# Softmax times V in column groups of 32 instead of 64, with the softmax sums formed apart from it

## The reference, cut to what matters

```python
x = _layernorm(x + _L0_attn_ref(x, W_qkv, b_qkv))          # rotary self-attention, 16 heads of 32, full softmax
x = _layernorm(x + _L0_xattn_ref(x, ctx, ctx, ...))        # 12 gathered nodes of a tree over the context
x = _layernorm(x + _L0_ffn_ref(x, w1, b1, w2, b2))         # 512 -> 2048 -> 512, ReLU
```

```python
scores = jnp.einsum('bhqd,bhkd->bhqk', q, k) / math.sqrt(D)
w = jax.nn.softmax(scores, axis=-1)
out = jnp.einsum('bhqk,bhkd->bhqd', w, v)
```

## Time and profile before

| | us |
|---|---|
| median of 3 runs (2359.38 to 2368.48) | 2360.6 |
| the profiled execution | 2362.72 |
| its span, first to last instruction | 2360.7 |
| TensorE busy | 2049.5 (87%) |
| VectorE busy | 1616.1 (68%) |
| ScalarE busy | 1072.2 (45%) |
| GpSimd busy | 1036.9 (44%) |

### The profile page before, as it was taken

One profiled execution on the slowest core, in us unless ns is written; L12 is line 12 of the kernel. 1 busy time (PEld: TensorE's weight loads), 2 busy tenths in 40 slices (PEclk: granted clock), 3 DMA queues, 4 the chain that ended last, 5 costly groups with the idle time before them and its releaser, 6 DMA issues.

```text
span 2360.7 us, 33037 instructions
## 1 busy us (share of the span) xinstructions
PE 2049.5 (87%) x11360; PEld 1023.6 (43%) x11360; DVE 1616.1 (68%) x2129; ACT 1072.2 (45%) x1854; POOL 1036.9 (44%) x1084
## 2 busy tenths in 40 slices
PE   4899999999999999996147888998989999988997
PEld 2333333333333333331014555555555555555555
DVE  8564647566564647552568888888888888888850
ACT  3354545455555545464013444444444444444444
POOL 3232534244352535233444464465555555455420
PEclk9999999999999999998568999999999999999999
DMA  5442434434342434331875675665665675675520
GB/s 193 146 126 73 144 97 131 145 108 152 121 149 79 142 96 130 117 108 63 311 268 186 220 235 188 220 231 199 221 236 195 215 255 195 206 249 195 199 85 18
DMA packets 188800, 392.40 MB, mean 166 GB/s; under 512 B 20692, under 2 KB 82260, under 8 KB 188632
## 3 DMA queue, kind: packets, MB, share of 16 engines
q1 hardware_dynamic: 133336, 188.91, 25.1%
q0 software_dynamic: 55296, 201.35, 24.6%
HBM read 312.33 MB, written 77.59 MB: 165 GB/s over the span
## 4 chain that ended last, share of the span: by engine, by line
DVE 28%; DMA 11%; POOL 5%; issue 4%; PE 3%; ACT 0%; DVEq 0%; SPq 0%; ACTq 0%; POOLq 0%
DMA nb<-kv_flat,idx_rows 10%; DVE bank L1497 10%; DVE logits L1444 5%; POOL nb L1568 5%; DVE nb L1493 5%; DVE nb L1435 4%; PE bank L1172 1%; PE bank L1148 1%; DMA own<-kv_flat 1%; DVE bank L1503 1%; DVE logits L1448 1%; DVE own L1439 1%; DVE total L1474 1%; DVE top L1466 1%; DVE weights L1481 0%
## 5 line engine op out<-in xcount | busy, mean ns | idle before, releaser
L712 DVE TENSOR_REDUCE neg_max<-rows_ps 128x2 f32<-128x1024 f32 x256 | 312.4, 1220 | 298.3 <-PE rows_ps L499 298.2
L1568 POOL DMA_INDIRECT nb<-kv_flat,idx_rows x384 | 366.6, 955 | 138.0 <-issue 86.2
L1435 DVE TENSOR_TENSOR nb<-nb,bank 128x1024 f32<-128x1024 f32 x192 | 231.7, 1218 | 142.5 <-DMA nb<-kv_flat,idx_rows 137.7
L627 ACT ACTIVATE probsT<-e_ps 128x1024 f32<-128x1024 f32 x256 | 262.0, 1023 | 145.1 <-PE e_ps L527 144.8
L1596 POOL TENSOR_TENSOR nb<-nb,weights 128x1024 f32<-128x1024 f32 x96 | 182.5, 1914 | 281.8 <-DVE weights L1481 281.1
L1497 DVE TENSOR_TENSOR bank<-bank,nb 128x512 f32<-128x512 f32 x384 | 268.2, 698 | 24.7 <-DVE bank L1497 0.5
L1148 PE MATMUL bank<-x2T_hi,w_hi_sb 128*128 128x256 f16 x1024 | 282.4, 276 | 0.7 <-issue 0.7
L1148 PE MATMUL bank<-x2T_lo,w_hi_sb 128*128 128x256 f16 x1024 | 281.9, 275 | 0.0
L1148 PE MATMUL bank<-x2T_hi,w_lo_sb 128*128 128x256 f16 x1024 | 281.4, 275 | 0.0
L517 PE MATMUL o_ps<-probsT,v_sb 128*33 128x512 f32 x1024 | 269.6, 605 | 6.3 <-ACT oT L624 6.1
L1444 DVE TENSOR_REDUCE logits<-nb 128x32 f32<-128x1024 f32 x192 | 230.0, 1211 | 0.0
(11 more groups left out here) (158 smaller groups left out, 3611.8 us busy)
## 6 DMA issues: line engine op xcount, KB each, us to landing
kv_flat<-kv_nat SPq DMA_DIRECT2D x128, 256.0 KB, 3.3
own<-kv_flat SPq DMA_DIRECT2D x32, 512.0 KB, 3.8
q_stack<-qk_dram SPq DMA_DIRECT2D x96, 128.0 KB, 3.0
k_stack<-qk_dram SPq DMA_DIRECT2D x96, 128.0 KB, 3.3
piece<-in_pieces SPq DMA_DIRECT2D x40, 256.0 KB, 3.5
in_sb<-in_xT SPq DMA_DIRECT2D x8, 1024.0 KB, 6.6
in_sb<-in_ctxT SPq DMA_DIRECT2D x8, 1024.0 KB, 5.6
qk_dram<-hi SPq DMA_DIRECT2D x32, 256.0 KB, 2.2
```

Source lines behind the costliest of these rows:

```text
L627: act.activation(probsT[:, (d - E_LAG) % TT, :, :], e_ps[:], ACT.Exp, scale=1.0 / (Q_UP * K_UP))\
L712: dve.tensor_reduce(neg_max[:, g % 2, at:at + 2], rows_ps[:], AX.X, ALU.max, negate=True).then_inc(max_done, 1)
L1435: dve.tensor_tensor(kk, kk, q.unsqueeze(1).to_broadcast([P, GN, D]), ALU.mult)\
L1568: pool.indirect_dma_start(nb[:, slot(lt, g), k, :], None, kv_flat, bass.IndirectOffsetOnAxis(idx_rows[:, lt, at:at + 1], 0))\
```

## The change

The product with V takes four heads (a "quad") side by side, each with weights of 32 columns at partitions 0, 32, 64 and 96 of `o_ps`, in every second step. The exponentials of a quad's four key blocks come in the order block by block, two steps each. The column of ones is gone. The softmax sums are formed apart: the exponentials of the four key blocks are added up, in place in the buffer of one block, GpSimd adding the second block (128x2048, in steps 0, 8, 16 and 24) and VectorE the third and fourth (steps 2, 4, 10, 12, 18, 20, 26, 28). A new aux item "sum" (steps 5, 13, 21, 29) multiplies the result with 32 columns of ones, four heads side by side; ScalarE copies it (`sumT`), and one step later ("share") four fp32 matmuls with four columns of the identity turn it into the layout of the queries, of which VectorE takes the reciprocal. The step after that is the output turn, now once per quad, four per sequence. `probsT` holds three buffers of one block of four heads.

To make room in memory the rotation is done in place (`rot` is gone), so its first product waits for the shuffle and ScalarE's `raw` waits for GpSimd's low part; the tree's output has two buffers (`NAT`) instead of four. The tables of steps are rewritten: aux items, bounces, splits, normalisation, residual. The tail has 27 steps.

```diff
-TAIL = 25
+ADD_LAG = E_LAG + 4
+SUM_LAG = V_LAG + 7
+SHARE_LAG = SUM_LAG + 1
+OUT_LAG = SHARE_LAG + 1
+PROBS_PLACE = ((0, 1, 2, 1), (2, 1, 0, 1))
+TAIL = 27
-NAT = 4
+NAT = 2
-BOUNCE_NEXT = {12: 0, 16: 1, 25: 2, 31: 3}
+BOUNCE_NEXT = {11: 0, 15: 1, 29: 2, 31: 3}
-STACK_NEXT = {21: 0, 29: 1}
-X_SPLIT, CTX_LOAD, CTX_SPLIT, X_LOAD = 4, 12, 20, 25
-X1_SPLIT = {18: (0,), 19: (1,), 22: (2, 3)}
-X1_STORE, X_ROWS_LOAD, X_ROWS_BIAS = (20, 24), 24, 27
-RESIDUAL = 15
-LN_STEPS = {16: (("stats", 0), ("stats", 1)), 17: (("apply", 0), ("stats", 2)),
-            18: (("apply", 1), ("stats", 3)), 19: (("apply", 2), ("apply", 3))}
+STACK_NEXT = {21: 0, 30: 1}
+X_SPLIT, CTX_LOAD, CTX_SPLIT, X_LOAD = 2, 10, 22, 27
+X1_SPLIT = {20: (0,), 22: (1,), 24: (2, 3)}
+X1_STORE, X_ROWS_LOAD, X_ROWS_BIAS = (23, 26), 26, 30
+RESIDUAL = 16
+LN_STEPS = {17: (("stats", 0), ("stats", 1)), 19: (("apply", 0), ("stats", 2)),
+            21: (("apply", 1), ("stats", 3)), 23: (("apply", 2), ("apply", 3))}
+AUX_AT = {0: (("kv", 0),), 2: (("kv", 1),), 3: (("kv", 2),), 4: (("kv", 3),), 5: (("sum", 2),), 6: (("qk", 0),),
+          8: (("qk", 1),), 9: (("tree", 0), ("tree", 1)), 10: (("qk", 2),), 11: (("tree", 2), ("tree", 3)),
+          12: (("qk", 3),), 13: (("tree", 4), ("tree", 5), ("sum", 3)), 14: (("v", 0),),
+          15: (("tree", 6), ("tree", 7)), 16: (("kv", 4),), 17: (("kv", 5),), 18: (("kv", 6),), 19: (("v", 1),),
+          20: (("kv", 7),), 21: (("sum", 0),), 22: (("v", 2),), 23: (("v", 3),), 24: (("qk", 4),),
+          25: (("tree", 8), ("tree", 9)), 26: (("qk", 5),), 27: (("tree", 10), ("tree", 11)), 28: (("qk", 6),),
+          29: (("tree", 12), ("tree", 13), ("sum", 1)), 30: (("qk", 7),), 31: (("tree", 14), ("tree", 15))}
...
+                    elif kind == "sum":
+                        pe.wait_ge(probs_added, START + 2 * (b * QUADS + (i if i < 2 else i - QUADS) + 1))
+                        for side in range(QUAD):
+                            mm = pe.matmul(o[side * DH:(side + 1) * DH, :], ones[:],
+                                           probsT[:, PROBS_PLACE[i % 2][0], side, :], start=True, stop=True)
...
-                            for side in range(2):
-                                mm = pe.matmul(O[side * SIDE:side * SIDE + VW, :],
-                                               v_sb[:, slot, kt, 2 * pair + side, :],
-                                               probsT[:, (d - V_LAG) % TT, side, :], start=kt == 0, stop=kt == TT - 1)
+                            for side in range(QUAD):
+                                mm = pe.matmul(O[side * DH:(side + 1) * DH, :],
+                                               v_sb[:, slot, kt, quad % QUADS * QUAD + side, :],
+                                               probsT[:, PROBS_PLACE[quad % 2][kt], side, :],
+                                               start=kt == 0, stop=kt == TT - 1)
...
+                            for t in range(TT):
+                                mm = pe.matmul(MB[:, t * QUAD:(t + 1) * QUAD], sumT[:, t * P:(t + 1) * P], heads,
+                                               start=True, stop=True)
...
+                            if kt < 2 and side == 0 and not (first and quad == 0):
+                                act.wait_ge(probs_added, START + 2 * n - 1 + kt)
+                            if kt == 3 and side == 0:
+                                act.wait_ge(first_added, START + n + 1)
...
+                            dve.wait_ge(e_done, START + n * PER_CHUNK + 2 * kt + 2)
+                            if kt == 2:
+                                dve.wait_ge(first_added, START + n + 1)
+                            else:
+                                dve.wait_ge(probs_added, START + 2 * n + 1)
+                            summed = probsT[:, place[0]].rearrange("p h t -> p (h t)")
+                            dve.tensor_tensor(summed, summed, probsT[:, place[kt]].rearrange("p h t -> p (h t)"),
+                                              ALU.add).then_inc(probs_added, 1)
...
+                            pool.wait_ge(e_done, START + n * PER_CHUNK + 4)
+                            pool.wait_ge(probs_used, START + 3 * n + 1)
+                            summed = probsT[:, place[0]].rearrange("p h t -> p (h t)")
+                            pool.tensor_tensor(summed, summed, probsT[:, place[1]].rearrange("p h t -> p (h t)"),
+                                               ALU.add).then_inc(first_added, 1)
```

More of the change, by code:

```diff
@@ L60 @@
 ROW_SCALE = 4096.0
-ONES = DH
-VW = DH + 1
-SIDE = 64
 M_ROW = 3 * DH
@@ L68 @@
 GROUP = 16
-PAIRS = H // 2
+QUADS = H // 4
+QUAD = 4
 STEPS = TT * H // 2
@@ L97 @@
[L97 to L121, removed]
-    before = 2 * KC if first else len(aux_order(True, False)) + 2 * KC - len(aux_order(False, False))
-    return before + (0 if first else b * len(aux_order(False, False))) + aux_place(kind, i, first, last)
+STACK_NEXT = {21: 0, 30: 1}
@@ new lines, with aux_items, aux_order @@
+V_FIRST = {0: (0, 1), 1: (2,), 2: (3,)}
+def aux_items(d, first, last, tail=False):
+    own = tuple(("v0", i) for i in V_FIRST.get(d, ())) if first else ()
+    late = d < SUM_LAG
+    return own + tuple(item for item in AUX_AT.get(d, ())
+                       if not (last and item[0] in ("qk", "v")) and not (first and item[0] == "sum" and late)
+                       and not (tail and (item[0] != "sum" or not late)))
+def aux_order(first, last, tail=False):
+    return [item for d in range(STEPS) for item in aux_items(d, first, last, tail)]
@@ new lines, in aux_place, with aux_number @@
+def aux_place(kind, i, first, last, tail=False):
+    return aux_order(first, last, tail).index((kind, i))
+def aux_number(b, kind, i, first, last, tail=False):
+    whole = len(aux_order(False, False))
+    if first:
+        behind = 2 * KC
+    elif tail:
+        behind = 2 * KC + len(aux_order(True, False)) + (b - 2) * whole + len(aux_order(False, True))
+    else:
+        behind = 2 * KC + len(aux_order(True, False)) - whole + b * whole
+    return behind + aux_place(kind, i, first, last, tail)
@@ L140, in max_group, with share_turn @@
     return (d // PER_CHUNK - 1) % KC
+def share_turn(d, first, tail):
+    return quad_step(d, SHARE_LAG, first, tail)
 def out_turn(d, first, tail):
-    return d % TT == V_LAG % TT and not (first and d < V_LAG + TT) and not (tail and d > V_LAG)
+    return quad_step(d, OUT_LAG, first, tail)
 def misc_order(first, tail):
-    return [(kind, d) for d in range(TAIL if tail else STEPS) for kind, turn in (("max", max_turn), ("out", out_turn))
+    return [(kind, d) for d in range(TAIL if tail else STEPS) for kind, turn in (("max", max_turn), ("share", share_turn), ("out", out_turn))
             if turn(d, first, tail)]
@@ L521, in iteration @@
+                        for kind, i in aux_items(d, first, last, tail):
+                            if kind == "sum":
+                                aux(b, kind, i, first, last, tail)
                         if e_step(d, first, tail):
-                            pair, kt = divmod((d - E_LAG) % STEPS, TT)
+                            quad, at = divmod((d - E_LAG) % STEPS, PER_CHUNK)
+                            kt, pair = at // 2, 2 * quad + at % 2
                             if (d - E_LAG) % PER_CHUNK == 0:
```

134 lines of the change are left out of this document (76 added, 58 removed).

## The result

The changed kernel took 2349.6 us (median of six runs, 2333.5 to 2354.4), the kernel before beside it 2363.3: ratio 0.9922, 95% interval 0.9899 to 0.9945. The same file in a second job gave 2343.5 against 2357.7: 0.9936 (0.9911 to 0.996). So it is faster, by about 14 us; the forecast was 36.

What follows compares the result with a forecast made beforehand. TensorE's own instructions were taken to set the pace. Six steady periods -31 us, iteration 0 -4, last iteration -6, tail +5: total -36, from a median of 2360.6 to 2325 us, range 2275 to 2382.

Steps and rivals of the forecast that it cites:

- The product's pitch: TensorE's product with V: four heads side by side at a pitch of 1.05 us, against 0.98 for two.
- rival 4: TensorE's column groups run two and two, product 1.96 us, period 141, total 2428 us; chance 0.07.
- the period: One steady batch: 116.0 us of TensorE work plus 11 of stalls, 127.0 against 132.1.
- the walk of steps 9 to 13: Stalls of 1.1 us before step 9, 0.6 before 11, 0.5 before 12, 1.0 before 13, together 3.2.
- the three meetings with GpSimd in steps 23, 25 and 31: GpSimd delays VectorE: 1.5 us for normalisations of 23, 1.2 for the rotation of 25, 1.1 for that of 31.
- Rival 3: GpSimd's additions hold VectorE's two-input operations: 143 us a batch, +63 in all, half of it 2375; chance 0.12.
- rival 1: VectorE's slack takes in rotations and additions, stalls stay at 6 us: period 122, total 2290; chance 0.12.
- Rival 2: Gain just eaten: stalls of 15 to 19 us a batch, total within 12 us of the median; chance 0.09.
- The walk: Step by step through a batch: rotations and additions in neighbouring steps stall TensorE by 3.2, 3.6 and 1.0 us.
- Last iteration, -6 forecast: Last iteration: steps without a projection held at 1.96 us by the maximum's loop, so not -10 but -6 us.
- None comes near: SP queue moves, including stores with two buffers for four: nothing charged; stores land after 3.3 us, tree-turn pairs 6 apart.
- Tail, +5 forecast: Tail: addition, sum, its copy and share behind the last exponential, 2.2 + 1.1 + 0.6 + 0.9, about +5 us.

Runs made afterwards that it cites:

- run 4: Changed kernel with all twelve additions of exponentials per sequence cut to 16 of 2048 columns, waits kept: 2308.1 us, 0.9784.
- run 3: Changed kernel with the last sequence's load of x's rows behind the last tree stores and its bias in step 1 of the tail: 2337.1 us, 0.9909.
- run 8: Changed kernel with mended ends: loads as in run 3, VectorE making all three tail additions, GpSimd's bias waiting for the first quad's: 2330.8 us, 0.9857.
- run 12: Mended ends of run 8 plus unread row scores in the tail, behind the scores of steps with a product: 2328.4 us, 0.9881.
- Run 2: Kernel before the change with two buffers for the tree's output instead of four, nothing else: 2388.4 us, 1.0132.
- the first kind of fill: Unread row scores in the tail, placed ahead of the products: 2326.8 us, 0.9882 with mended ends; 2336.4 us, 0.9923 with the change's own ends.
- run 7: Changed kernel with only GpSimd's additions cut to 16 columns: 2315.4 us, 0.9835; with only VectorE's cut: 2311.0 us, 0.9809.

## Why the prediction was wrong in size

**Right.** The product's pitch (1.00 for 1.05, rival 4 is out), the sums and shares, VectorE's addition (2.3 where nothing holds it), the period (126.2 and 127.1 for 127.0), iteration 0, the walk of steps 9 to 13, and the three meetings with GpSimd in steps 23, 25 and 31. Rival 3 is out, as no period came near 133; rival 1 too, since VectorE's slack didn't swallow anything. Rival 2 came near in the total, but not by its cause: stalls were 11.6 us a batch, not 15 to 19. GpSimd's addition took 4.56 for 4.1. In rival 4 the terms as written add up to 2433, not 2428.

**Right, but not additive.** The walk charged 7.8 us of stalls to rotations and additions side by side, and run 4 finds 8.1 at the steps of the additions. Yet without them the period is only 3.5 us shorter: behind these stalls stand others, above all the tree's two buffers, which they cover. The normalisations of step 23 were taken at 1.5 and cost 2.3.

**Last iteration, -6 forecast, +7 measured.** Two steps failed. "None comes near", said of the SP queue, took a store's landing to be 3.3 us, the median. A store behind a load of 1 MB frees its buffer later: in the last iteration the load of x stands ahead of four stores, TensorE waits 5.5 us for the sum's buffer (which the prediction named as a sign of being wrong), and the loss is 6 to 7.5 us (runs 3 and 8), less where TensorE comes later (run 12). Run 2 shows that the term deserved a price anywhere. The other 5.5 us: even mended it gains nothing (95.9 for 96.2). The -6 counted no hold by GpSimd there, but step 23 with its normalisations takes 5.2 us where the kernel before has 2.7, and step 25 is 1.6 longer. It also took the clock to stay at 1.00, and the mended last iteration has 0.95. How the 5.5 us divide among these isn't shown.

**Tail, +5 forecast, +10.5 measured.** The forecast put its +5 behind the last exponential and nothing ahead of it. Us from the last maximum to the last exponential, and from there to the first gather:

| | to the last exponential | behind it | clock up to it |
|---|---|---|---|
| before | 22.8 | 33.8 | 1.00 |
| forecast | 22.8 | 38.8 | 1.00 |
| after | 30.3 | 36.9 | 0.82 |
| mended ends (8) | 28.7 | 39.1 | 0.82 |
| mended ends, tail filled (12) | 25.6 | 37.2 | 1.00 |

Behind the last exponential the chain came to +3.1, less than forecast. The step that failed is one that was never written down: that the exponentials of the tail keep their old pace, and TensorE its clock of 1.00. They came 7.5 us later. Part of it is there at clock 1.00 too (2.8 us in the filled tail). Part is half clock: scores, products, sum and turns on the chain take about double, 5 us in the mended tail (run 12). Part is GpSimd's additions, for which two exponentials of after wait, 1.3 and 1.1 us; at clock 1.00, with the first kind of fill in both, the tail is 1.0 us longer with them (67.4 for 66.3). From these, 1.1 us of the missing 5.5 are the filled tail above the forecast (62.8 for 61.7), 1.0 the additions, and the remaining 3.4 the clock. That is an estimate: no run fills the change's own tail without pushing its scores back. And that the filled tail meets the forecast's total so well is in part luck, as 2.8 us too few ahead of the last exponential stand against 1.6 too many behind it.

Together 13 + 5.5 = 18.5 us at the end of the stage, of the 22 between forecast (-36) and measured medians (-14). The rest is within what executions differ by in the steady part (757 to 763) and in the second stage.

## What to carry to other kernels

Cost the first and last iteration with the same care as the steady one: they have other neighbours on each queue, and a term that is nothing in the steady part (two buffers for four) can be 6 us there. Look at what stands ahead of a store on its queue, and not only at how long the store itself takes. Where an edit takes TensorE work out of a chain in which it takes turns with another engine, ask what its clock does in the gaps; work that nobody reads, put where it waits anyway, took 5 us off the tail here. Put ahead of something that others wait for, it gave most of that away again. And where an engine has hardly any idle time over several steps, moving work among these steps only moves the stall.

## What was not expected of the hardware

- Short dips to granted clock 0.5 in a stage in which TensorE is busy for 93% of the time. They begin at or behind its waits of about 2 us for VectorE, and all but one are gone with 1.3 to 1.7 us of useless matmuls in those waits (0.98 to 1.00).
- The same TensorE work at the same starts for 18 us, and then half clock in one kernel and full clock in the other (runs 7 and 8).
- Four column groups of fp32, eight records, in the pitch of two (1.00 for 0.98).
- GpSimd and VectorE, each with two operands in memory, nearly add up: 9.05 us for 4.95 beside 4.58.
- A store of 256 KB behind a load of 1 MB on the same queue held its buffer so long that ScalarE waited 6.8 us; with the load behind the stores it waited at most 2.3.
